# Self-attention of a two-layer transformer: where a step's value matmuls stand in TensorE's order

## The reference

```python
h = _layernorm(x, ln1_g, ln1_b)
q, k, v = h @ wq, h @ wk, h @ wv           # 16 heads of 64
attn = einsum('bihd,bjhd->bhij', q, k) * scale
attn = softmax(attn, axis=-1)
out = einsum('bhij,bjhd->bihd', attn, v).reshape(B, S, 1024)
x = out @ wo + bo + x
```

## Time and profile before

| | |
|---|---|
| median of 3 runs | 2356.99 us (2356.91 to 2363.16) |
| the profiled execution | 2367.88 us, its span 2366.2 us |
| mean granted TensorE clock | 0.979 of full |
| busy | PE 91%, PEld 61%, DVE 74%, ACT 62%, POOL 49% |
| score steps, exponential pairs | 512 |
| max matmuls and reductions | 1024 |
| value matmuls | 3 lines x 4096 |
| gathers, shifts | 128, 64 |

### The profile page before, as it was taken

The page is one execution under the profiler, slowest core; times in us unless marked ns, Lnnn a source line. Parts: engine busy times, 40 slices in busy tenths (PEclk is TensorE's granted clock), DMA queues, the critical chain, the costliest instruction groups (busy, mean ns, idle before and its releaser), DMA issues.

```text
span 2366.2 us, 59153 instructions
## 1 busy us (share of the span) xinstructions
PE 2162.7 (91%) x25392; PEld 1445.5 (61%) x25392; DVE 1744.3 (74%) x3148; ACT 1477.7 (62%) x1948; POOL 1156.2 (49%) x730
## 2 busy tenths in 40 slices
PE   4999999899899999889989999989998999998999
PEld 1566566575556666567556666656755666666675
DVE  5888887467588888655758888865576888885664
ACT  2788788244288887823538878772353888785442
POOL 3666675133076766612316766652232667663231
PEclk8999999899999999989999999999999999999999
DMA  3221220000132222001023123100103223210000
GB/s 105 70 71 51 65 69 25 10 22 31 46 105 54 60 73 59 22 5 37 23 66 88 51 70 80 42 26 1 37 16 85 69 60 84 58 35 20 10 10 18
DMA packets 60165, 114.19 MB, mean 48 GB/s; under 512 B 9344, under 2 KB 21632, under 8 KB 59904
## 3 DMA queue, kind: packets, MB, share of 16 engines
q1 hardware_dynamic: 59904, 110.41, 17.2%
HBM read 55.72 MB, written 4.19 MB: 25 GB/s over the span
## 4 chain that ended last, share of the span: by engine, by line
PE 63%; DVE 21%; ACT 9%; issue 4%; POOL 1%; DMA 1%; POOLq 0%; SPq 0%; ACTq 0%; DVEq 0%
PE work L831 7%; PE scores L861 6%; DVE minima L1396 6%; PE scores L746 6%; PE scores L854 6%; PE scores L748 6%; PE scores L747 6%; DVE prob L1411 4%; PE work L746 4%; PE work L747 3%; PE work L748 3%; ACT prob L1199 3%; PE work L883 3%; PE work L879 3%; PE work L881 3%
## 5 line engine op out<-in xcount | busy, mean ns | idle before, releaser
L693 POOL TENSOR_TENSOR prob<-prob 128x1024 f16<-128x1024 f32 x256 | 584.9, 2285 | 557.2 <-ACT prob L1200 546.2
L1396 DVE TENSOR_REDUCE minima<-work 128x1 f32<-128x512 f32 x1024 | 679.7, 683 | 45.0 <-PE work L831 31.4
L1199 ACT ACTIVATE prob<-scores 128x1024 f32<-128x1024 f32 x512 | 525.8, 1027 | 130.9 <-PE scores L861 113.8
L1200 ACT ACTIVATE prob<-scores 128x1024 f16<-128x1024 f32 x512 | 522.8, 1021 | 0.0
L879 PE MATMUL work<-vals,prob 128*128 128x65 f16 x4096 | 429.9, 193 | 15.5 <-POOL prob L693 13.3
L879 PEld LDWEIGHTS work<-vals,prob 128*128 128x128 f16 x4096 | 383.6, 99 | 78.1 <-POOL prob L693 14.9
L883 PE MATMUL work<-vals,prob 128*128 128x65 f16 x4096 | 430.4, 195 | 0.0
L881 PE MATMUL work<-vals,prob 128*128 128x64 f16 x4096 | 430.3, 193 | 0.0
L881 PEld LDWEIGHTS work<-vals,prob 128*128 128x128 f16 x4096 | 380.6, 97 | 58.2 <-issue 0.3
L831 PE MATMUL work<-ka,qa 128*128 128x512 f16 x1024 | 391.1, 387 | 24.8 <-DVE minima L1396 18.4
L883 PEld LDWEIGHTS work<-vals,prob 128*128 128x128 f16 x4096 | 381.0, 97 | 0.0
(11 more groups left out here) (160 smaller groups left out, 4196.6 us busy)
## 6 DMA issues: line engine op xcount, KB each, us to landing
qa<-staged_q SPq DMA_DIRECT2D x128, 128.0 KB, 2.3
ka<-staged_k SPq DMA_DIRECT2D x128, 128.0 KB, 2.3
raw_even<-in_pairs SPq DMA_DIRECT2D x32, 384.0 KB, 3.4
raw_odd<-in_pairs SPq DMA_DIRECT2D x32, 384.0 KB, 3.3
raw_odd<-in_pieces SPq DMA_DIRECT2D x20, 512.0 KB, 3.7
raw_even<-in_pieces SPq DMA_DIRECT2D x20, 512.0 KB, 3.7
qb<-staged_q SPq DMA_DIRECT2D x64, 128.0 KB, 2.3
kb<-staged_k SPq DMA_DIRECT2D x64, 128.0 KB, 2.3
```

Of the source, the lines that this page charges most:

```text
L693: pool.tensor_tensor(prob[1][:, slot, :], prob32[:, slot, :], prob[0][:, slot, :], ALU.subtract).then_inc(a.polished, 1)
L1199: act.activation(prob32[:, n % RING, :], source, ACT.Exp)
L1200: act.activation(prob[0][:, n % RING, :], source, ACT.Exp)\
L1396: dve.tensor_reduce(minima[:, t, h:h + 1], out[:, :], AX.X, ALU.max, negate=True)\
```

## The change

One step of the list is moved. The value step that stood at the end of step s, behind the second max and the low half, now stands at its very start, ahead of the shift, the first max, the placed steps and score s. The gather that belongs to it stays where it was, at the end of the step behind the low half. Nothing is added or removed: the same instructions run on every engine, and the index of the value step that goes with step s is the same (s - 3).

```diff
     for s in range(TILES):
         peaks = [step for step in peaks_of[s] if step.kind == "max"]
+        behind_values = value(s - LAG, par, head) if s >= LAG else value(TILES - LAG + s, *prv) if before else []
+        out += behind_values[:1]
         if s == TILES - 1 and after:
             out.append(Step("shift", 0, *nxt, 0))
...
         elif before:
             out += low(TILES - 1, *prv)
-        if s >= LAG:
-            out += value(s - LAG, par, head)
-        elif before:
-            out += value(TILES - LAG + s, *prv)
+        out += behind_values[1:]
     return out
```

## The result

The changed kernel takes 2615.5 us, against 2357.0 us before: 1.109 times as long, with a 95% interval of 1.107 to 1.111. The forecast was 2630 us with a range of 2535 to 2700.

A forecast was written before the change was run, and what follows sets the result against it. PE was taken as the bound, so its waits lengthen the span: 188 us of waits plus 85 us of clock falls, 273 us, on the 2357 us median gave 2630 us, range 2535 to 2700 us.

The forecast's parts named there:

- step 2: Behind the second max, value 0 waits for value 7's gather: 1.68 us (even units), 2.00 us (odd), 56 places.
- step 6: Behind the last max, value 4 waits for value 3's gather, so the shift starts later: 60 x 1.24 = 74 us.
- stall for GpSimd's low half: Value 3 in odd units comes 0.8 us too early; 0.4 us taken, times 27 = 11 us.
- falls of the clock: PE's granted clock falls behind the new gaps: 14 + 36 = 50 falls x 1.7 = 85 us, bounds 0 and 150.
- VectorE's low halves are done well before the slot: In the moved value step's slot, DVE's low halves are ready early; no wait was put for them.
- The first unit of a round, the last one and the semaphore's 0.1 us: Step 2's first unit has no unit before, last put at nothing (bound 0.6 us); semaphore 0.1 us per gather wait.
- PE's matmuls follow each other without slack: Inside a unit PE feeds itself, so a microsecond in which it stands still is one of the span.
- Only the waits, no falls: Rival, on PE's clock: the new waits cost 188 us and the clock doesn't fall; 2545 us, 13%.
- Half of the waits come back: Rival, over a unit: PE isn't the bound, DVE or ScalarE gives back half of 188, no falls; 2451 us, 6%.
- The gather is done when PE comes: Rival, at value 4: the shift's wait falls away without another, 60 x 1.17 = 70 us; 2287 us, 2%.
- The move does nothing: Rival, at the output bank: the semaphore's count for an empty bank is already met when PE comes; 2357 us, 2%.
- over 2700 us: Rival, on PE's clock: more falls, or falls outlasting one stretch, with the low half's stall in full; above 2700 us, 7%.

The follow-up runs named there:

- the fillers: The changed kernel with 4 (step 2) or 5 (step 6) further matmuls on TensorE ahead of the wait for the gather; 2540.3 us, ratio 1.077.

## Why the prediction was right

**The steps that held.** That a value step comes one slot earlier and meets its gather, which is queued behind reductions, is the mechanism that the experiments show. The terms against the profile of after:

| term | forecast | measured |
|---|---|---|
| step 2 | 47 + 56 = 103 us | 103.5 us |
| step 6 | 74 us | 73.9 us |
| stall for GpSimd's low half | 11 us net of up to 22 | waits +19.9 us, 12.2 of them where forecast |
| falls of the clock | 50, 85 us | 35, 55 us |
| sum | 273 us | 243.7 us between profiles, 258.6 between medians |

By kind, step 2 was 1.68 and 2.00 us per unit and came out at 1.70 and 1.98. Step 6 was 1.24 and 1.25, and that its sum was met so closely is luck, for two misses cancel: in the 32 even units it cost 1.39 each on average, more than forecast because value 4 took 0.82 us up to the shift where 0.75 was put (831.75 to 832.57 above) and longer still where the clock had fallen by then. In the 28 odd ones it was 1.05, and in most of these 0.83 (2.99 against 2.16), since the stall at value 3 gives VectorE time to catch up. That stall came in 18 of the odd units, 0.65 us in most, and not in 27. In 9 of the others VectorE's low half of step 2 lasted 2.2 to 2.5 us instead of 1.22, and value 2 waited for it (5.9 us); that VectorE's low halves are done well before the slot was wrong there. The first unit of a round, the last one and the semaphore's 0.1 us (0.15 in truth) were too small to matter. That PE's matmuls follow each other without slack, so that a wait is a loss in full, is shown by the runs that take the gathers out of the way: what PE no longer waits comes back in the time.

**The term that was mis-sized: the falls.** The waits alone were forecast at 188 us, and the profiles' difference without the clock's 54.7 is 189.0. So what was off is the clock, 85 us against 55. Against the profiles the forecast is 29 us too high, and that it is only 14 off against the medians comes from which executions were profiled. The forecast had a fall behind 6 in 10 of the 60 gaps of step 6 and behind half of the odd gaps of step 2, and none behind the gaps of 1.5. Behind the last it was 0 of 28. In step 2 of odd units (1.88 us) it was 10 of 28. In step 6 the two kinds of unit differ: behind the even units' 28 gaps of 2.37 to 2.45 us there were 26 falls, and behind the odd ones' 32 gaps a single one. The forecast had the odd gaps at 2.3 us. Sixteen of them were 1.77 us, shortened by the stall that comes 4 us ahead of them; that the two overlap was in the text, but the clock was reckoned with the longer gap. The shortening isn't the whole reason, though, for ten odd gaps were 2.17 to 2.34 us long and only one of these had a fall. The trace shows how these ten differ: nine lie in a unit in which the clock had already fallen behind the gap of step 2, and these are the nine units in which VectorE's low half of step 2 was late and value 3 didn't stall. The tenth had no fall at step 2, and it is the one with a fall at step 6. So no odd unit had a fall at both steps. Why stays open, as does what decides behind gaps of equal length. The shares were also read from two gaps too few. The trace of before has a gap of 1.72 us at L861 (at 983.84) with no fall, and one of 1.85 us at L879 (at 2166.79) with a fall 2.8 us later, behind a second gap of 1.41. They would have changed the shares little. The cost of a fall was 109.4 / 35 = 3.1 us at the low level, 1.6 us lost, against the forecast's 1.7.

**The rivals.** *Only the waits, no falls*, 2545 us: it is what the fillers made, 2540.3 us. The kernel itself had the falls. The rule of thumb of the Trainium skill that the prediction names ("TensorE: Matmul & The Clock Gate", section "HAM oscillation — how this bites in real kernels"), by which gaps this short cost nothing, did not hold for it: 38 falls came behind gaps of 1.6 to 2.5 us. *Half of the waits come back*: no, the two profiles' difference is the full sum. *The gather is done when PE comes*: it ended 2.67 us behind the start of the last max in the even unit shown, as before. *The move does nothing*, and *over 2700 us*: neither; the changed kernel came near the latter when VectorE was delayed further (2697.7).

## What to carry to other kernels

When a step is moved ahead in one engine's order, look at which buffer it takes and where the instruction that frees it stands in the other engine's queue: here an emptying of 0.63 us cost 0.8 to 2.0 us each time, for what was queued ahead of it. An engine's wait that is shown for one instruction is not won by changing that instruction; the wait at the shift was VectorE's queue, and it fell from 70.5 to 24.9 us when work that wasn't urgent left that queue (2357 to 2316 us). A gap costs twice if TensorE's clock falls behind it, and here a gap partly filled with useless matmuls was cheaper than an idle one.

## What was not expected of the hardware

- Whether the clock falls isn't told by the length of one gap. Gaps of 1.77 us in step 6 of odd units had a fall behind none of 16 in the changed kernel and, with the gather of step 2 by its value, behind 16 of 23 of the same length. In the kernel with the gather of step 6 by its value, 9 falls came behind gaps of 1.04 us that were followed by a second one at the shift.
- A TensorE that stood idle began 0.15 us after the gather's end, one that had just run fillers 0.06 us after it.
- One GpSimd subtraction of 2.12 us held a VectorE subtraction for 1.35 us (2.57 instead of 1.22), and with this in 24 of 32 even units, moving GpSimd's work by two steps cost 82 us. The kernel before has long ones too, where they cost less: VectorE's low half of step 6 in odd units was over 1.6 us long in 31 of 32, with a mean of 2.01 us, in the changed kernel in 3.
